# Node features first: reordering the loads and the setup of a graph layer, with the table blocks begun after 12 columns

## What is computed

```
xn  = layernorm(x)                                   # 1250 x 512
xs  = xn[:, :128] @ W_in2f_s ; xv = xn[:, 128:] (as 128 x 3) @ W_in2f_v
u   = edge_attr_3 / |edge_attr_3|                    # per edge
W   = (shifted_softplus(edge_attr_20 @ Wf1 + bf1) @ Wf2 + bf2) * rcut
m   = products of xs[idx_j], xv[idx_j], u and W      # per edge
agg = segment_sum(m, idx_i)                          # per node
x   = x + (two small layers of agg)
x   = x + experts(layernorm(x))                      # top-k tokens per expert
```

## Time and profile before

| | us |
|---|---|
| median of 3 runs (1441.02 to 1441.79) | 1441.53 |
| the profiled execution | 1442.35 |
| its span in the trace | 1440.5 |
| PE / DVE / ACT / POOL busy | 1323.8 / 1027.4 / 816.6 / 799.3 |

### The profile page before, as it was taken

How to read it: one execution, slowest core, us unless ns; L and a number is a source line. 1 busy time by engine, 2 the same in 40 slices (tenths; PEclk the granted TensorE clock), 3 DMA queues, 4 the chain that set the end, 5 groups by cost and what they waited for, 6 DMA issues and landing times. The chain is left out here.

```text
span 1440.5 us, 26692 instructions
## 1 busy us (share of the span) xinstructions
PE 1323.8 (92%) x7075; PEld 791.9 (55%) x7075; DVE 1027.4 (71%) x2512; ACT 816.6 (57%) x2049; POOL 799.3 (55%) x843
## 2 busy tenths in 40 slices
PE   5786799999999999999999999999962799999997
PEld 1463456656555556555555555555561455555553
DVE  7869589999999899999999999998776311111110
ACT  3769667777777777777777777777550111111111
POOL 5258577777777777777777777777200122222211
PEclk7689899999999999999999999999995799999998
DMA  7315033444443444444443333434452155555421
GB/s 246 162 44 162 20 113 113 123 130 123 126 127 110 129 124 127 127 132 136 123 115 109 110 114 109 115 109 112 65 189 71 58 164 163 163 163 162 145 37 18
DMA packets 65870, 172.45 MB, mean 120 GB/s; under 512 B 14260, under 2 KB 22820, under 8 KB 65191
## 3 DMA queue, kind: packets, MB, share of 16 engines
q0 software_dynamic: 43424, 105.53, 27.9%
q1 hardware_dynamic: 22398, 66.38, 13.4%
HBM read 148.53 MB, written 18.08 MB: 116 GB/s over the span
## 5 line engine op out<-in xcount | busy, mean ns | idle before, releaser
L1130 PE MATMUL PS<-prod,oneh 128*64 128x256 f32 x2052 | 469.6, 382 | 4.0 <-DVE region_s L944 2.0
L564 POOL DMA_INDIRECT recs<-rec_d,inv_i x342 | 323.2, 945 | 113.0 <-issue 81.0
L575 POOL DMA_INDIRECT gath<-table_d,recs x342 | 323.5, 946 | 106.0 <-issue 78.7
L1130 PEld LDWEIGHTS PS<-prod,oneh 128*64 128x64 f32 x2052 | 268.9, 137 | 199.4 <-issue 77.7
L707 ACT ACTIVATE oneh<-oneh,recs 128x64 f32<-128x64 f32 x1026 | 282.2, 338 | 145.7 <-DVE oneh L921 143.8
L1123 PE MATMUL PS<-prod,oneh 128*64 128x256 f32 x1368 | 356.1, 392 | 0.0
L1111 PE MATMUL PS<-wf_sb,h_t 128*128 128x512 f32 x684 | 333.2, 610 | 2.9 <-DVE h_t L907 2.9
L932 DVE TENSOR_TENSOR prod<-PS,gath 128x768 f32<-128x768 f32 x342 | 324.9, 950 | 0.0
L944 DVE TENSOR_TENSOR region_s<-region_s,PS 128x512 f32 x342 | 232.6, 680 | 17.9 <-issue 13.6
L714 ACT COPY PS<-c_rep 128x512 f32<-128x512 f32 x338 | 190.4, 583 | 79.0 <-DVE prod L932 78.6
L930 DVE TENSOR_TENSOR prod<-PS,gath 128x256 f32<-128x256 f32 x342 | 143.9, 421 | 54.6 <-DMA gath<-table_d,recs 38.7
(11 more groups left out here) (264 smaller groups left out, 1503.8 us busy)
## 6 DMA issues: line engine op xcount, KB each, us to landing
region_r<-wu SPq DMA_DIRECT2D x16, 512.0 KB, 4.3
region_r<-wd SPq DMA_DIRECT2D x16, 512.0 KB, 5.6
region_u<-wu SPq DMA_DIRECT2D x16, 512.0 KB, 4.3
region_u<-wd SPq DMA_DIRECT2D x16, 512.0 KB, 5.8
recs<-rec_d,inv_i POOLq DMA_INDIRECT x342, 2.6
gath<-table_d,recs POOLq DMA_INDIRECT x342, 3.3
region_u<-rec_in SPq DMA_DIRECT2D x1, 5168.0 KB, 16.1
rec_d<-region_u SPq DMA_DIRECT2D x1, 5168.0 KB
```

The lines of the kernel that those rows point to most:

```text
L564: nc.gpsimd.indirect_dma_start(out=recs[:, q % RING, k, :], out_offset=None, in_=rec_d, in_offset=bass.IndirectOffsetOnAxis(ap=inv_i[:, t: ...
L575: nc.gpsimd.indirect_dma_start(out=gath[:, t % GRING, :], out_offset=None, in_=table_d, in_offset=bass.IndirectOffsetOnAxis(ap=recs[:, q % ...
L1130: return nc.tensor.matmul(to, oneh[:, slot, 1 + i, :], prod[:, slot, P_Q:P_B + i + 1:1 + i, :], start=i == 0, stop=i == 2, skip_group_chec ...
```

## The change

- SP: x stands right behind `src`; the records stand behind the weights.
- GpSimd: `weights` ahead of `lengths`. `directions` waits for the second root instead of the first.
- DVE: `node_variance` ahead of bucket 9 and `node_scales` ahead of bucket 12 of `pick_places`, instead of behind columns 18 and 24. The reciprocal of the edge lengths behind column 32, instead of ahead of bucket 10.
- ScalarE: the root of the edge lengths and the first two `evacuate_x` stand behind the normalisation and ahead of the first batches of slots.
- PE: the first two `transpose_x` stand ahead of the columns, with waits for the picks whose banks they reuse. 12 columns instead of 24 ahead of the table.
- Shares: ScalarE takes slots from column 12 (was 24); it takes 5 of 9 columns from 132 to 269 (was from 144 to the end) and 4 of 9 otherwise. GpSimd's share is as before, from column 48.

```diff
-ALONE = 24
-LATE = 144
+ALONE = 12
+LATE = 132
+LAST_BUSY = 270
 def by_scalar(n):
-    return n >= ALONE and n % 9 in ((1, 3, 5, 7) if n < LATE else (1, 3, 5, 7, 8))
+    return n >= ALONE and n % 9 in ((1, 3, 5, 7, 8) if LATE <= n < LAST_BUSY else (1, 3, 5, 7))
 def by_pool(n):
-    return n >= 2 * ALONE and n % 9 in (0, 4)
+    return n >= 48 and n % 9 in (0, 4)
@@ SP
                 sp.dma_start(src_i, src).then_inc(s_src, 16)
-                sp.dma_start(unsorted, rec_in).then_inc(s_edges, 16)
+                for cut in CUTS:
+                    sp.dma_start(x_sb[cut], x.rearrange("(p t) h -> p t h", t=BLOCKS)[cut]).then_inc(s_x, 16)
                 sp.wait_ge(s_wready, 1)
...
-                for cut in CUTS:
-                    sp.dma_start(x_sb[cut], x.rearrange("(p t) h -> p t h", t=BLOCKS)[cut]).then_inc(s_x, 16)
+                sp.dma_start(unsorted, rec_in).then_inc(s_edges, 16)
@@ GpSimd
-                    pool.wait_ge(s_rt, 1)
+                    pool.wait_ge(s_rt, 2)
...
+                weights()
                 lengths()
-                weights()
                 directions()
                 constants()
@@ ScalarE
-                act.wait_ge(s_sq, 1)
-                nc.scalar.activation(squares[:, 0, :], squares[:, 3, :], ACT.Sqrt).then_inc(s_rt, 1)
                 act.wait_ge(s_x, 16 * len(CUTS))
...
                 nc.scalar.activation(rstd[0:BP, 1, :], rstd[0:BP, 0, :], ACT.Sqrt).then_inc(s_rt, 1)
-                slot_batches(0, 2)
                 act.wait_ge(s_norm, 1)
...
+                act.wait_ge(s_sq, 1)
+                nc.scalar.activation(squares[:, 0, :], squares[:, 3, :], ACT.Sqrt).then_inc(s_rt, 1)
+                evacuate_x(0)
+                evacuate_x(1)
+                slot_batches(0, 2)
                 act.wait_ge(s_cps, 2)
                 nc.scalar.copy(c_raw, ps_d[0:1, :]).then_inc(s_cps, 1)
-                evacuate_x(0)
-                evacuate_x(1)
@@ DVE, pick_places
-                        if b == BUCKETS // 2:
-                            dve.wait_ge(s_rt, 1)
-                            nc.vector.reciprocal(squares[:, 1, :], squares[:, 0, :]).then_inc(s_recip, 1)
+                        if b == 9:
+                            node_variance()
+                        if b == 12:
+                            node_scales()
@@ DVE, node_scales
-                    dve.wait_ge(s_rt, 2)
+                    dve.wait_ge(s_rt, 1)
@@ DVE, columns
                     column_one_hots(j)
-                    if j == ALONE - 6:
-                        node_variance()
-                    if j == ALONE:
-                        node_scales()
+                    if j == OH_RING:
+                        dve.wait_ge(s_rt, 2)
+                        nc.vector.reciprocal(squares[:, 1, :], squares[:, 0, :]).then_inc(s_recip, 1)
@@ PE, transpose_x
-                    if t >= 2:
+                    if t < 2:
+                        pe.wait_ge(s_place, BUCKETS - len(ps_place) + 1 + t)
+                    else:
                         pe.wait_ge(s_xte, t - 1)
@@ PE, the list
+                transpose_x(0)
+                transpose_x(1)
                 pe.wait_ge(i_name, 1)
                 for j in range(ALONE):
                     add_column(j)
-                transpose_x(0)
-                transpose_x(1)
```

## The result

The change gains a quarter of what was forecast. The median is 1437.3 us over ten runs (1434.84 to 1439.12) against 1440.41 for the kernel before in as many: ratio 0.9978, interval 0.9968 to 0.9987. That is 3.1 us where 12.55 were forecast, and above the upper end of the range, 1435. The profiled execution took 1438.67 with a span of 1436.7; for the kernel before these are 1442.35 and 1440.5. These two executions differ by 3.7 us, the spans by 3.8.

What follows compares the result with a forecast made beforehand. The last column's matmul was taken to release the edge loop, with the table late because x is late. Terms -14.0 + 1.25 + 0.7 - 0.5 = -12.55 us gave a median of 1429.0, range 1425.5 to 1435.

Steps and rivals of the forecast that it cites:

- x first ... I take 12.5: Load of x in front: arrival at 12.5 us, between 9.1 and 17.0; sums end at 25.8, DVE waits 1.3.
- upper bound of 17.0: Latest arrival of x if its load in front still takes the 15.7 us it took behind the records.
- about 1.4 us of scales: Time forecast for DVE's scales among the picks, which were to end at about 33.8 us.
- Rival A: x still late, at 17.0; DVE stands at bucket 9, picks end at 38.7; gain 7.7, 1433.9 us; chance 0.15.
- DVE among the picks: Variance and scales among DVE's picks: picks end at about 33.8, column 0 at about 35.8, 0.9 us earlier.
- Ahead of the table: From the columns ahead to the table's start: first table block at 43.5 against 57.54, -14.0 us.
- The rounds: Ten rounds of a table block and 12 columns: 53.6 us kept, 0; directions +0.7 and clock -0.5 counted separately.
- +0.7 for the directions: Loss while GpSimd's directions hold DVE during the columns: between 0 and 6.1 us, taken as +0.7.
- Rival B: GpSimd's directions hold DVE and PE feels all 6.1 us instead of 0.7; gain 7.2, 1434.4 us; chance 0.12.
- Rival D: TensorE stays at 1.2 GHz through the ten rounds: +20.8 us, 1449.8; chance 0.03.
- The rest: After the tenth table copy: 26 Relus left instead of 25, ScalarE's 49.5 becomes 51.5, together +1.25 us.
- rival E: No change: something other than the last column, such as the later records, releases the edge loop; chance 0.03.

Runs made afterwards that it cites:

- e3_lengths_held: Changed kernel with GpSimd starting the edge lengths only when the scales are done; ratio 0.9967 to the kernel before.
- e1_x_alone: Changed kernel with SP waiting until x has landed before it issues the weights and the records; ratio 0.9972 to the kernel before.
- e5_x_in_pairs: Changed kernel with x loaded in five pairs of blocks, a semaphore each, sums starting per pair; ratios 0.9945 and 0.9922 to the kernel before.
- e2_scales_behind: Changed kernel with DVE's variance ahead of bucket 16 and its scales behind the last pick; ratio 0.9942 to the kernel before.
- before_again: The kernel before, run once more without a change; ratio 0.9997.
- e8_pairs_0_ahead: Changed kernel with x loaded in pairs of blocks and no column ahead of the table; ratio 0.9884 to the kernel before, 1626.52 against 1643.01 us.
- e4_no_directions: Changed kernel without GpSimd's five operations that make the unit vectors, so the edge vectors stay unscaled; ratio 0.9965 to the kernel before.
- e7_24_ahead: Changed kernel with 24 columns ahead of the table and ScalarE's shares from 24 and 144; ratio 0.9973 to the kernel before.

## Why the prediction was wrong

**"x first ... I take 12.5": the step that failed.** x could be used at 16.0 (15.6 to 16.8 in the nine executions that load it this way), near the upper bound of 17.0, and the gain of the first block was 7.9 instead of 14.0. Of the miss of 6.1 us, DVE's stall at bucket 9 is 3.9 (5.20 against the 1.3 forecast) and the held scales 2.3 to 2.6 (3.7 us against the 1.4 forecast; 2.6 recovered by `e3_lengths_held`); the path behind them is as forecast. x is slow with nothing behind it too (`e1_x_alone`): some 10 us to move and at least 3.3 more until ScalarE can start. I had put 4.5 of the 7.9 us between 15.7 and 7.8 down to queueing; the move to the front took off 1.0. The second step that failed is the "about 1.4 us of scales", which measured 3.7 beside `lengths`.

The whole miss adds up: the span became 3.8 us shorter where 12.5 were forecast, and of these 8.7 us the first block makes 6.1, the rounds 1.7, the last stretch 0.5 and the part behind the names 0.4.

**Rival A** named the mechanism and its place, the wait at the variance, and had the upper bound of x. It fell short: the picks ended at 40.2 and not 38.7 although x came a microsecond sooner than it says, as it left out the scales that GpSimd holds.

**DVE among the picks.** I saw that the records would land at about 30 and that GpSimd's multiplications hold DVE, and asked for it at `split_places` only. With x later, the scales lay on `lengths`. With the data there, the place among the picks gives column 0 at 34.61 (`e5_x_in_pairs`), 2.0 us sooner than before; without it, at 41.97, 5.3 us later than in `e2_scales_behind`.

**Ahead of the table** was right: 7.6 us from column 0 to the block, 7.7 forecast. The 43.33 of `e2_scales_behind` is two small misses that cancel.

**The rounds.** Forecast +0.2, measured +1.9 in the profiled executions. PE's busy time makes +2.0 of it (48.32 against 46.29, granted clock 0.81 against 0.84) and PE's idle time -0.1. Three executions of the changed kernel have a mean of 54.1 us and two of before 52.9, and they overlap. That the change lengthens the rounds isn't shown. The +0.7 for the directions was too much if anything: PE's idle time shows nothing of them. Rival B isn't what happened: DVE is held, but PE waits for ScalarE's slots. DVE's lead at the first block fell from 24 columns to 7, which the forecast doesn't mention, and it sufficed. Rival D didn't happen.

**The rest** was right in count, 26 Relus, and 0.5 us short in size (+1.73, forecast +1.25). Behind the names the program took 1278.1 and 1278.5 us. From `before_again` to `e8_pairs_0_ahead`, on one chip, the names came 17.5 us sooner (160.27, 142.80) and the span was 17.9 shorter. So moving the moment of the names moved the end nearly one for one, and rival E fell; single executions stray from it: behind the names `e1_x_alone`, `e2_scales_behind` and `e4_no_directions` took 3.2 to 3.6 us more than the changed kernel, and `e7_24_ahead` some 10 more than the others on its chip.

**Still open:** why the granted clock over the rounds is 0.81 in one execution and 0.90 in another of one program. The first four variants had 0.84, 0.85, 0.92 and 0.93. No run here separates a cause, so the profiled +1.94 couldn't have been forecast from such a trace. Open too is why x moves at 256 GB/s and what it waits for behind its last byte.

## What to carry to other kernels

When a load is moved to the front so that an engine in the midst of other work can use it, don't place the consumer by the load's size: take what the same load took in the trace as the likely case, and put the consumer behind work that runs anyway, where a late arrival costs nothing. Better, load in parts with a semaphore each: here ScalarE starts on the first part at 7.8 us instead of on the whole at 16.0, and the work hides the rest. And after moving a load back, look at what now starts with its arrival, and which small operations of the neighbouring engine lie in those microseconds. Before putting a longer or shorter stretch of matmuls down to a change, split the stretch into PE's busy and idle time and read the granted clock beside it.

## What the runs showed that was not expected

- A DMA's bytes had all moved by 12, and its consumer, with nothing else to do, started at 15.32 (`e1_x_alone`).
- Moving ScalarE's root behind the sums put a table load of 1.28 us (L643 at 29.30) between them and the reciprocal of the deviation. It was hidden here, as DVE was in its picks until 31.4.
- The same ten rounds of one program took 51.7 to 55.6 us, at granted clocks of 0.90 and 0.81: 3.9 us, more than the whole gain of the change. PE's busy time differs by 4.3.
- The profile put PE's wait at 62.31 down to a DVE operation. The end of ScalarE's Relu, 0.14 us ahead of each such matmul, shows that it was ScalarE.
- Twelve columns fewer ahead of the table left DVE 7 columns ahead of PE at the first block instead of 24, and this was still enough to cover a held operation of 2.10 us.
